# A decoder block with a top-2 mixture: rows written to per-expert regions while they are routed, instead of gathered after routing

## The reference

```python
# 1: a causal sum with rotors (Wk isn't used)
v = x @ Wv.T
rotors = exp(1j * t * freqs)
x = layernorm(x + real(cumsum(v * rotors) * conj(rotors)) @ Wo.T)
# 2: attention to ctx with a decay matrix, no softmax
s = einsum('bsd,btd->bst', x, ctx) / 16 * decay
s = s / maximum(abs(sum(s, -1)), 1)[:, None, :]
x = layernorm(x + einsum('bst,btd->bsd', s, ctx))
# 3: mixture of 8 experts, two for each token
probs = softmax(x @ router_w.T); scores, idx = top_k(probs, 2); scores /= sum(scores)
h = einsum('nh,ehd->end', x, up_proj)                  # 256 -> 512
out_e = einsum('end,edh->enh', silu(h[..., :256]) * h[..., 256:], down_proj)
x = layernorm(x + sum over the two chosen experts of score * out_e)
```

## Time and profile before

| | |
|---|---|
| median of 3 runs | 262.0 us (261.5 to 263.92) |
| the profiled execution | 263.22 us, of which the span of the profile is 261.4 us |
| busy in the span | PE 207.2, DVE 161.7, ACT 111.1, POOL 146.5 us |
| moved by DMA | 35.75 MB, 137 GB/s in the mean |
| instructions | 5197 |

### The profile page before, as it was taken

One profiled execution on the slowest core, in us unless ns is written; L12 is line 12 of the kernel. 1 busy time (PEld: TensorE's weight loads), 2 busy tenths in 40 slices (PEclk: granted clock), 3 DMA queues, 4 the chain that ended last, 5 costly groups with the idle time before them and its releaser, 6 DMA issues.

```text
span 261.4 us, 5197 instructions
## 1 busy us (share of the span) xinstructions
PE 207.2 (79%) x1365; PEld 182.3 (70%) x1366; DVE 161.7 (62%) x534; ACT 111.1 (42%) x277; POOL 146.5 (56%) x156
## 2 busy tenths in 40 slices
PE   8578999999999997756999999999999999300000
PEld 8467798898998896745888988888888888200000
DVE  4765888889887684954454544454545454017993
ACT  2233144244234113541454545454545555425665
POOL 0064775676666410565576777777777774415340
PEclk9999999999999999979999999999999999955555
DMA  7962674775671012801222323233232341089323
GB/s 196 384 228 67 251 230 144 270 222 151 230 240 45 0 44 82 280 3 60 80 93 89 100 85 100 88 99 100 85 100 88 102 97 61 11 263 327 134 88 153
DMA packets 20130, 35.75 MB, mean 137 GB/s; under 512 B 2861, under 2 KB 11312, under 8 KB 20112
## 3 DMA queue, kind: packets, MB, share of 16 engines
q1 hardware_dynamic: 16368, 26.21, 30.1%
q0 software_dynamic: 3744, 9.31, 11.7%
HBM read 27.12 MB, written 9.31 MB: 139 GB/s over the span
## 4 chain that ended last, share of the span: by engine, by line
PE 63%; DVE 16%; DMA 6%; POOL 5%; issue 5%; ACT 2%; SPq 1%; DVEq 1%; ACTq 0%; POOLq 0%
PE p_c L545 14%; PE p_v L545 7%; PE p_y L467 5%; PE p_v L411 4%; PE p_y L571 4%; PE p_r L545 4%; PE p_c L427 4%; PE p_a L545 3%; PE p_s L545 3%; PE p_t L584 3%; POOL space L999 3%; PE p_s L451 3%; DVE space L838 3%; PE p_a L486 2%; PE p_r L495 2%
## 5 line engine op out<-in xcount | busy, mean ns | idle before, releaser
L545 PE MATMUL p_c<-w_hi,parts 128*128 x104 | 34.6, 414 | 0.0
L1023 POOL DMA_INDIRECT y_dram<-x1T,scatter_now x26 | 26.3, 1013 | 11.9 <-issue 6.5
L1003 POOL DMA_INDIRECT turns<-x_dram,gather_now x26 | 25.5, 979 | 12.6 <-issue 3.8
L969 POOL TENSOR_TENSOR w_lo<-keep,w_hi 128x384 fp32r<-128x384 f32 (+1 forms) x32 | 31.3, 999 | 0.0
L981 POOL TENSOR_TENSOR space<-back 128x512 f32<-128x512 f32 x8 | 10.1, 1268 | 30.9 <-DVE back L704 30.9
L810 DVE TENSOR_TENSOR parts<-p_y,parts 128x256 fp32r<-128x256 f32 x39 | 16.5, 423 | 17.7 <-ACT parts L912 17.7
L820 DVE TENSOR_TENSOR cs<-p_c,cs 128x256 f32<-128x256 f32 x26 | 11.0, 424 | 22.7 <-ACT cs L919 22.7
L919 ACT ACTIVATE cs<-p_c 128x256 f32<-128x256 f32 x26 | 10.0, 385 | 24.7 <-PE p_c L545 24.7
L545 PEld LDWEIGHTS p_c<-w_hi,parts 128*128 128x128 f32 x104 | 17.6, 189 | 2.3
L1034 POOL TENSOR_TENSOR space<-space,keep 128x512 f32<-128x512 f32 (+1 forms) x8 | 10.4, 1298 | 15.0 <-ACT space L941 15.0
L912 ACT ACTIVATE parts<-p_y 128x256 fp32r<-128x256 f32 x39 | 14.8, 380 | 8.8 <-PE p_y L571 8.6
(11 more groups left out here) (153 smaller groups left out, 552.0 us busy)
## 6 DMA issues: line engine op xcount, KB each, us to landing
keep<-in_weights SPq DMA_DIRECT2D x8, 768.0 KB, 4.8
space<-y_dram SPq DMA_DIRECT2D x16, 256.0 KB, 4.0
space<-in_xT SPq DMA_DIRECT2D x8, 256.0 KB, 3.1
keep<-in_x SPq DMA_DIRECT2D x8, 256.0 KB, 2.8
space<-in_ctxT SPq DMA_DIRECT2D x8, 256.0 KB, 5.2
space<-in_ctxt SPq DMA_DIRECT2D x8, 256.0 KB, 4.9
x_dram<-x SPq DMA_DIRECT2D x8, 256.0 KB, 4.7
keep<-x_dram SPq DMA_DIRECT2D x1, 2048.0 KB, 8.2
```

Of the source, the lines that this page charges most:

```text
L545: last = nc.tensor.matmul(dst, lhs[:, k, :], w[:].rearrange("p e n -> p (e n)")[:, bass.ds(start + col + k * width, width)], start=(n == 0 ...
L969: return nc.gpsimd.tensor_tensor(w_lo[:, bass.ds(e, 1), :].rearrange("p a n -> p (a n)")[:, n], w_in[s][:, n], whole[:, n].bitcast(F32), A ...
L1003: nc.gpsimd.indirect_dma_start(xs[s], None, x2_dram, bass.IndirectOffsetOnAxis(ap=gather_now[s][:], axis=0)).then_inc(xs_ok[s], 16)
L1023: nc.gpsimd.indirect_dma_start(y_dram, bass.IndirectOffsetOnAxis(ap=scatter_now[s][:], axis=0), ys[s], None, bounds_check=TOPK * N - 1, oo ...
```

## The change

- Each expert has a region of 17 tiles in DRAM (`rows_dram`). As soon as the experts of four sequences are known, POOL writes their x2 rows to their places there, one indirect DMA for each sequence and choice (32 in all, `send`). A row is 258 words: x2, the place of its result, and a code of its first choice.
- Routing runs in four groups of four sequences, in the same small DVE operations: groups 0 and 1 in steps 4 to 7, group 2 in step 8 and around tiles 0 to 2, group 3 in tiles 3 to 8. TensorE places a group with six small matmuls in the row sums' bank.
- The tiles come in three phases (9, 8 and 22 tiles), each a list of tiles that the groups so far have filled: phase 0 needs groups 0 and 1, phase 1 group 2, phase 2 group 3. What is left in a region's last tile is filled with rows that are skipped. SP loads tiles with plain DMAs, four buffers deep; there are no gathers, one-hot matrices or inversion.
- x2 stays in SBUF (`x2_rows`); it isn't stored in order and loaded again.
- In the pair loop x2 is normalised by ACT, from `rs2` and a new `shift2`; `att` is divided by `vinv` on ACT (`att_div`) instead of the context on POOL; `w_hi` comes right after the first square root; `w_lo` is one operation for an expert, a step earlier, and waits for x2 of its step.
- `y_dram` has both rows of a token beside each other, one 512 KB load a pair; loops on TensorE, DVE and POOL and the tile loops are unrolled; two down banks instead of three; Exp and the gates come after the last tile.

```diff
-DVE_ROWS, POOL_ROWS, ACT_ROWS = range(0, 11), range(11, 20), range(20, TOPK * B)
+REGION = TOPK * N // 2 // P + 1
+GROUPS = ((0, 4), (4, 8), (8, 12), (12, B))
+ROW = D + 2
+SENDS = {5: ((0, 0), (0, 3)), 6: ((3, 4), (4, 6)), 7: ((6, 7), (7, 9)), 8: ((0, 0), (9, 16))}
...
# SP
+            def load_tile(k):
+                g, kk = phase_of[k], in_phase[k]
+                if k >= XS:
+                    sp.wait_ge(xt_ok, k - XS + 1)
+                    sp.wait_ge(put_idx_ok, k - XS + 1)
+                if kk == 0:
+                    sp.wait_ge(table_ok, g + 1)
+                    sp.wait_ge(rows_ok[g], 16 * TOPK * (GROUPS[g + 1][1] - (GROUPS[g + 1][0] if g else 0)))
...
+                if 11 <= k < 11 + E // 2:
+                    sp.wait_ge(fill_at_ok, 1)
+                    for e in (2 * (k - 11), 2 * (k - 11) + 1):
...
+                at = sp.value_load(row_idx[g][0:1, kk:kk + 1], min_val=0, max_val=E * REGION * P)
+                sp.dma_start(xs[k % XS], rows_dram[bass.ds(at, P), :]).then_inc(xs_ok[k % XS], 16)
...
# TensorE, pair loop
+            def place(g):
...
+                for b in range(n):
+                    last = nc.tensor.matmul(p_place[:, b + 1:n + 1, :], half[:, H_ONES:H_ONES + P],
+                                            chosen[:, first + b:first + b + 1, :].to_broadcast([P, n - b, E]),
+                                            start=False, stop=True, skip_group_check=True)
...
+                if i in (5, 7):
+                    pe.wait_ge(logits_ok, i - 2)
+                    place((i - 5) // 2)
...
-                        last = nc.tensor.matmul(p_a[:, q, :], att[:, q, :], cs[:, q, :], start=True, stop=True)
+                        last = nc.tensor.matmul(p_a[:, q, :], att_div[:, q, :], c_in[1 - s][:, q, :], start=True, stop=True)
...
# TensorE, tiles
+                if k == 0:
+                    pe.wait_ge(logits_ok, PAIRS)
+                    place(2)
+                if k == 5:
+                    pe.wait_ge(place_read, 3)
+                    place(3)
...
# DVE, pair loop: place_in_step 0 is ahead of att, 2 is ahead of turned
+            def at_step(i, place_in_step):
+                where = (i, place_in_step)
+                for g in (0, 1):
+                    if where == (4 + 2 * g, 0):
+                        choose(g, 0)
+                    if where == (4 + 2 * g, 2):
+                        choose(g, 1)
+                        mark(g)
+                    if where == (5 + 2 * g, 0):
+                        destinations(g)
+                if where == (7, 2):
+                    dve.wait_ge(zeros_ok, 7)
+                    count_tiles(0)
+                if where == (8, 0):
+                    choose(2, 0)
+                if where == (8, 2):
+                    list_tiles(0)
...
-                    normalise(i - 2, r2, mv2, sd2, rs2, x2[s], sd2_ok, rs2_ok, x2_ok)
+                    dve.wait_ge(sd2_ok, i - 1)
+                    nc.vector.reciprocal(rs2[:], sd2[:]).then_inc(rs2_ok, 1)
+                    dve.wait_ge(rs2_ok, i - 1)
+                    nc.vector.scalar_tensor_tensor(shift2[:], mv2[:, :, 0], -1.0, rs2[:], ALU.mult, ALU.mult).then_inc(
+                        shift2_ok, 1)
...
# DVE, tiles, behind the tile's own operations
+                if k == 0:
+                    destinations(2)
+                if k == 1:
+                    pass_over(0)
+                    count_tiles(1)
+                if k == 2:
+                    list_tiles(1)
+                if k == 3:
+                    choose(3, 0)
+                if k == 4:
+                    choose(3, 1)
+                    mark(3)
+                if k == 6:
+                    destinations(3)
+                if k == 7:
+                    pass_over(1)
+                    count_tiles(2)
+                if k == 8:
+                    list_tiles(2)
...
# ACT, pair loop, behind the square root for x2
+                    act.wait_ge(shift2_ok, i - 1)
+                    for q in range(2):
+                        last = nc.scalar.activation(x2_pair(i - 2)[:, q, :], r2[:, q, :], ACT.Identity,
+                                                    scale=rs2[:, q:q + 1], bias=shift2[:, q:q + 1])
...
+                    act.wait_ge(vinv_ok, i)
...
+                        last = nc.scalar.activation(att_div[:, q, :], att[:, q, :], ACT.Copy, scale=vinv[:, q:q + 1])
...
# POOL, pair loop
+            def send(first, end):
+                for n in range(first, end):
+                    b, c = n // TOPK, n % TOPK
+                    g = b // 4
+                    if n % (4 * TOPK) == 0:
+                        pool.wait_ge(dest_ok, g + 1)
+                    nc.gpsimd.indirect_dma_start(
+                            rows_dram, bass.IndirectOffsetOnAxis(ap=dest_idx[:, c, b:b + 1], axis=0),
+                            x2_rows[:, b, :], None, bounds_check=E * REGION * P - 1, oob_is_err=False).then_inc(
+                                rows_ok[max(g - 1, 0)], 16)
...
+                    pool.wait_ge(hi_ok, i + 1)
+                    if i >= 5:
+                        send(*SENDS[i][0])
                     if has(-2):
...
+                        pool.wait_ge(x2_ok, i - 1)
+                    nc.gpsimd.tensor_tensor(w_lo[:, bass.ds(i, 1), :].rearrange("p a n -> p (a n)"), w_in[s],
...
+                if i >= 5:
+                    send(*SENDS[i][1])
...
# POOL, tiles, behind the scatter of tile k-2
+                if k in (1, 2, 3, 4):
+                    send(2 * k + 14, 2 * k + 16)
+                if k in (7, 8, 9, 10):
+                    send(2 * k + 10, 2 * k + 12)
```

More of the change, by code:

```diff
@@ L143, in decoder_block @@
         att = sb("att", [P, 2, T])
+        att_div = sb("att_div", [P, 2, T])
         vabs = sb("vabs", [P, 2])
@@ L152, in decoder_block @@
         rs2 = sb("rs2", [P, 2])
-        x2 = [sb(f"x2_{s}", [P, 2, D]) for s in range(2)]
+        shift2 = sb("shift2", [P, 2])
+        x2_rows = sb("x2_rows", [P, B, ROW])
         x2T = sb("x2T", [P, 2, KC, T])
@@ L199, in decoder_block @@
[L199 to L207, removed]
@@ L208, in decoder_block @@
-        expert_idx = sb("expert_idx", [P, TILES], I32)
-        xs = [turns[:, 0, :], turns[:, 1, :], rem[:, 0, :]]
+        placed = sb("placed", [P, TOPK, B, E])
+        dest = sb("dest", [P, TOPK, B])
+        dest_idx = sb("dest_idx", [P, TOPK, B], I32)
+        ends = [sb(f"ends{g}", [P, E]) for g in range(3)]
+        part = sb("part", [P, E])
+        done = sb("done", [P, E])
+        first_tile = [const[:, C_FIRST:C_FIRST + E + 1]] + [sb(f"first_tile{g}", [P, E + 1])[:] for g in (1, 2)]
@@ new lines, in destinations @@
+            def destinations(g):
+                first, end = GROUPS[g]
+                b = slice(first, end)
+                n = end - first
+                dve.wait_ge(place_ok, g + 1)
+                if g > 0:
+                    link(nc.vector.tensor_copy(ends[g - 1][:], p_place[:, n, :]))
+                link(nc.vector.tensor_tensor(placed[:, :, b, :], pick[:, :, b, :],
+                                             p_place[:, 0:n, :].unsqueeze(1).to_broadcast([P, TOPK, n, E]), ALU.mult))
+                dve.sem_inc(place_read, 1)
+                link(nc.vector.tensor_reduce(dest[:, :, b], placed[:, :, b, :], AX_X, ALU.add))
+                link(nc.vector.tensor_copy(dest_idx[:, :, b], dest[:, :, b]))
+                dve.sem_inc(dest_ok, 1)
+                if g == 3:
+                    nc.vector.tensor_copy(fill_idx[:], ends[2][:]).then_inc(fill_at_ok, 1)
@@ new lines, in count_tiles @@
+            def count_tiles(g):
+                starts = first_tile[g]
+                bias = HALF if g == 2 else -HALF
+                link(nc.vector.tensor_scalar(part[:], ends[g][:], bias, 1.0 / P, ALU.add, ALU.mult))
+                link(nc.vector.tensor_scalar(done[:], part[:], ROUND, -ROUND, ALU.add, ALU.add))
+                link(nc.vector.tensor_tensor(upto[0][:, E:], done[:], starts[:, 0:E], ALU.subtract))
+                link(nc.vector.tensor_tensor(jump[:], starts[:, 1:E + 1], done[:], ALU.subtract))
+                for m in range(3):
+                    by = 2 ** m
+                    link(nc.vector.tensor_tensor(upto[m + 1][:, E:], upto[m][:, E:], upto[m][:, E - by:2 * E - by], ALU.add))
@@ L800, in _ @@
+            tiles(tile)
             dve.wait_ge(exp_ok, 1)
@@ L882, in step @@
                     nc.scalar.activation(vabs[:], rowsum, ACT.Abs).then_inc(vabs_ok, 1)
[L883 to L886 removed]
+                    act.wait_ge(vinv_ok, i)
+                    if has(-2):
+                        act.wait_ge(av_ok, i - 1)
+                    for q in range(2):
+                        last = nc.scalar.activation(att_div[:, q, :], att[:, q, :], ACT.Copy, scale=vinv[:, q:q + 1])
+                    last.then_inc(cs_ok, 1)
                 if has(-2):
@@ L1018, in tile @@
+            for i in range(PAIRS + 1):
+                step(i, i % 2, lambda k: 0 <= i + k < PAIRS)
```

(5 more changed lines are left out.)

512 lines of the change are left out of this document (218 added, 294 removed).

## The result

The changed kernel takes 273.0 us (median of 4 runs, 270.98 to 273.7) beside 262.0 before: a ratio of 1.039, 95% interval 1.033 to 1.046. The prediction was 255.9, faster; it came out slower. The profiled execution took 272.9 us with a span of 271.1. Medians are of all executions of a kernel, while the ratios and their intervals leave out those over 1.5% above its fastest, so a ratio isn't quite the quotient of two medians.

A forecast was written before the change was run, and what follows sets the result against it. TensorE was taken to bound pair and tile loops, with a 19.6 us gap before the first tile copy to win back; first tile -8.85, tile stage +3.75, finish -1.0 made -6.1, so 262.0 became 255.9 us, range 250.0 to 262.0.

The forecast's parts named there:

- a first tile later than 117 us: Sign that would prove the sum wrong; ACT's first tile copy was forecast near 112.8 us.
- Routing in the steps: Pair loop, DVE's small operations: +2.95 us each in steps 4 and 6, +0.75 in 5 and 7, +1.3 in 7, -1.4 in 8 and 9.
- Pair steps without routing: Pair loop: x2 on ACT makes vmax start later, +0.3 us a step, +1.8 over six steps.
- The send: POOL's indirect DMA of x2 rows: about 1.0 us busy, 1.30 us a send, ends 1.2 and 1.8.
- Rival B: Slower because the send is dear: 0.5 us more each (1.8) gives 265.5 us; chance 0.10.
- First tile: Between last logits and tiles: tile 0 there near 111.5 us, ACT's copy near 112.8 instead of 121.65, -8.85 us.
- Tile stage: Tile loop: +1.45 DVE blocks, +0.6 placements, +2.5 late tile 9, -0.8 unrolled; in sum +3.75 us.
- The wait for tile 9: Tile loop: third group's rows land late, so TensorE waits 2.5 us for tile 9's load (0 to 6).
- The steady pace of 2.54: Tile loop: TensorE sets 2.54 us a tile; unrolling removes four tiles of 2.81, -0.8 us.
- Rival C: TensorE's clock falls to 1.2 GHz at tile 9 and once in steps 4 to 7: 259.9 us; chance 0.10.
- Finish: After the tiles: y as one 512 KB load a pair, no x2 reload; -1.0 us, ends +1 and -3.

The follow-up runs named there:

- e2: The changed kernel with POOL's low parts started only behind DVE's small routing operations of the step (vinv in step 1): 263.14 us, ratio 0.998.
- e5: The changed kernel with low parts behind the routing operations and one fill behind each of eight loads: 260.55 us, ratio 0.993.
- e4: The changed kernel with one filling store behind each load of tiles 9 to 16, not two ahead of tiles 11 to 14: 270.5 us, ratio 1.029.
- e8: The changed kernel with unread matmuls in TensorE's waits (11, 11, 9 and 9; steps 5, 7, 8 and the first tile): 269.05 us, ratio 1.024.
- e11: The kernel before, with POOL's addition of a pair in the finish waiting for DVE's second sum of the pair before: 260.8 us, ratio 0.993.
- e9: The changed kernel with low parts delayed, fills spread, sends earlier, fourteen fillers, and POOL's finish addition waiting for DVE's previous second sum: 255.56 us, ratio 0.972.
- e10: The kernel before with an expert's low part as one operation of 1536 columns instead of four of 384: 285.66 us, ratio 1.088.
- e1: The changed kernel with each expert's low part as four operations of 384 columns instead of one of 1536: 268.43 us, ratio 1.022.
- e12: The kernel of e9 with DVE's small shift in the finish moved ahead of the statistics: 256.76 us, ratio 0.979.

## Why the prediction was wrong

The profiled span was forecast at 255.3 us (261.4 less 6.1) and is 271.1. The 15.8 us stand in three places: the first tile copy 9.8 (122.60 against 112.8), the tile stage 4.6 (111.4 to the end of the last matmul, against 103.0 + 3.75), the finish 1.4. The prediction's own sign of a wrong sum, a first tile later than 117 us, came.

**Routing in the steps: the step that failed.** "Each small linked DVE operation takes 0.19 us and comes every 0.225", and the sums built on it. The rhythm itself was right: six operations ahead of `att` in step 4 take 1.36 us from 51.95 (forecast 1.35). What failed is that I took durations from a stretch in which POOL did nothing (102 to 105 us of the kernel before), and asked of POOL only whether somebody waits for it ("POOL loses 1.2 us a step, which nobody waits for"). I did not ask what POOL's `w_lo`, moved to this place and made 3.45 us long, does to a DVE operation that starts under it. Five operations took 11.5 us more than their own time; the last logits came 9.75 us later than forecast (start 119.89, end 120.95 against 111.2). With four of the five holds gone (e2) they end at 108.4, below the forecast: steps 4 and 5 then take 11.3 and 11.2 us beside the 12.8 and 10.6 that I had.

A sign was in the rows I quoted: x2 took 1.08 us for two at 71.57, where x1, the same operation, takes 0.74, and I passed it as DVE's own cost. A piece of `w_lo` runs there from 71.18 to 72.18. A plainer one stands in the routing of the kernel before, in rows that I had not weighed: its first `ties` takes 0.63 us under POOL's `cs`, the second 0.26.

```profile
92.27 1.18 POOL L991 TENSOR_TENSOR cs<-space,vinv 128x256 f32<-128x256 f32 x2 [4.59 <-issue]
92.93 0.63 DVE L682 TENSOR_TENSOR ties<-logits,top 128x96 f32<-128x96 f32 x1
...
95.05 0.26 DVE L682 TENSOR_TENSOR ties<-masked,top 128x96 f32<-128x96 f32 x1
```

**Pair steps without routing: +0.3 a step, measured -0.17.** I set x2's 1.03 us on ACT against nothing but the start of `vmax`; x2 also left DVE, where part of its 1.08 was waiting for POOL. More than that, both steps keep TensorE full (9.57 of 9.57 us before, 9.40 of 9.40 after), so DVE's loop set neither of them, and a charge to that loop had nothing to lengthen. By the rows, 0.16 of the 0.17 lies in TensorE's product of `att` (1.11 us from 64.75 before, 0.95 from 46.02 after). Only step 3 can be read so: a hold in step 1 still delays step 2.

**The send: right.** 0.97 to 1.0 us busy and 0.30 to the next, so 1.28 beside 1.30. Rival B, the slower one, was priced on this and did not come; the loss came from a mechanism that I had not listed. Nor did sends hold DVE's small operations here: `ties` at 107.00 takes 0.19 under a send of 106.67 to 107.64 (for exceptions see the last section).

**First tile: right in its form.** Copy 1.7 us after the logits, forecast 1.6. In e2 and e5, with the logits early, TensorE waits 2.0 us for tile 0's load: sends and load are then the later of the two, as the estimate of 111.5 us for them had it (110.43 in e2).

**Tile stage.** The wait for tile 9 was right (2.42, forecast 2.5). From the transposes of tile 1 to the place where those of tile 9 were due, TensorE took 2.7 us more than eight steady tiles, forecast 2.05; tiles 9 to 14 took 3.4 more than six steady ones (149.00 to 167.60 us), forecast nothing. The steady pace of 2.54 in unrolled tiles was right. Missing were SP's fills, which stand in no term of the sum (e4: 2.5 us), and the clock at the first tile (0.70 from 123.5 to 129.2). Rival C had the clock right as a mechanism; it came in steps 5, 7 and 8 and at the first tile, and cost about 4 us (e8), in part behind waits that the holds made.

**Finish: -1.0, measured +0.4.** The load of y rows is 1.5 us shorter, as hoped; what it frees, POOL's addition over DVE's sum takes. The term was sized from "the rest is DVE, POOL and ACT at their pace", as if that pace were a constant of each engine. e11 shows that the kernel before had the same loss there, about 2 us.

**What the change was worth.** Its idea holds: with four orders mended (low part, fills, sends, the finish) and fourteen fillers, in e9, it is 2.8% faster than before, 255.56 us, close to what I forecast for it as it stood (255.9). That agreement is luck and no credit to the sum: the holds were missing in it, and the terms for the steps, with and without routing, were too dear. The order in the finish helps the kernel before as well (e11), so 0.7 of the 2.8% isn't the change's own.

Of the clock nothing is left in e9: it is 1.00 in every window from 40 to 130 us. A hold is left there: x1 takes 1.89 us at 94.49, under a `w_lo`. What stays open is why the product of `att` is shorter in the changed kernel's step 3, and what part of e10's 23 us is due to the length of the operation.

## What to carry to other kernels

When an operation on POOL is moved or made longer, list what DVE starts in that time: one with two SBUF inputs, or a SBUF to SBUF tensor_scalar, costs the rest of POOL's instruction however small it is, and the cures are to start POOL's long operation behind DVE's small ones (9.9 us here) or to cut it into pieces (4.6 us). Take the durations of small operations from a stretch in which the neighbour engine does what it will do beside them, and read a row that takes longer than its twin elsewhere (1.08 against 0.74) as a question. Count a DMA on SP whose address is read from memory first as over a microsecond of its queue's time, as measured here, and put none between loads that an engine waits for.

## What the runs showed of the hardware

- One POOL operation of 1536 columns behind `got`, instead of one of 384 there and three earlier, made the kernel before some 23 us slower (e10). Pieces in a row don't hold as one: DVE gets in between two of them (`ties` 0.62 us instead of 3.05 in e1).
- The hold hits by operands, not by size: a 128x32 comparison 3.05 us, a 128x2 shift 1.17 us, and a 128x32 reduction 0.17, a 128x256 product with one input in PSUM 0.42, in the same company.
- It goes by who starts first, down to 0.03 us (e12), and both ways: POOL's addition at 258.48 in the changed kernel, 0.08 us behind the start of a DVE sum, takes 1.45 us instead of 1.18.
- Under POOL's indirect DMAs (0.97 us each) DVE's small operations mostly keep their time: `ties` 0.19 us at 107.00, `vmax` 0.17 at 111.93. There are exceptions, and no run explains them. x1 at 74.30 takes 0.90 us instead of 0.73, and the DMA under it 1.15. In e1, `ties` at 75.56 starts in the last 0.25 us of such a DMA and 0.27 ahead of `got`, and still takes 1.61 us, to the end of `got`.
- On SP a load or fill at an address from a register came every 1.15 us in the mean (3.46 us for two fills and a load). The loads of y rows in the kernel before, whose addresses are fixed, were issued 0.41 to 0.51 us apart (228.21 to 229.63). That reading the address is what costs the difference is not isolated.
